# A fused attention and mixture-of-experts layer: normalised rows kept as half-precision pairs and turned by DMA instead of by TensorE

## The chip, the cores and the metric

The kernel runs on one core of one Trainium2 chip. The metric is the device time in microseconds (us) of one execution; the median of several runs counts. The profile that is read here is of one profiled execution of the same program.

## The reference, cut to what matters

4096 tokens of 128 channels pass through a linear attention layer without softmax (16 heads of 8, rotary positions, a causal mask inside each 1024-token sequence, a gate and a layer norm), then a residual and a layer norm, and then a mixture of experts with two of eight experts per token and one shared expert, and again a residual and a layer norm:

```
x  = layernorm(x + attention(x))                    # called x1 below
logits = x1 @ gate_w                                # [4096, 8]
top_v, top_i = top_k(logits, 2);  top_p = softmax(top_v)
combine[t, e] = top_p of token t for expert e, else 0
g = x1 @ Wg[e];  u = x1 @ Wu[e];  d = (silu(g) * u) @ Wd[e]     # 352 inner
expert_out = sum over e of combine[:, e] * d
shared = (silu(x1 @ Sg) * (x1 @ Su)) @ Sd                       # 176 inner
out = layernorm(x1 + expert_out + shared)
```

## The kernel before

The work is cut into 32 tiles of 128 tokens, and four tiles in a row are a quad (R = 4). The five engines run programs of their own that wait for each other on semaphores; their order is written out by hand.

**Attention loop.** Steps s = 0 to 37 are software-pipelined: in step s TensorE (PE) runs `bank_p(s)`, then `proj(s + 3)`, `attend(s - 1)`, `energies(s)`, `products_of(s)` and `turn(s + 1)`. `bank_p` is all that goes into PSUM bank `b_p`: the router's logits of tile s - 5 (L558 to L560), the ranks of a quad's choices (L568 to L573), the transpose of the normalised tile s - 4 (L580), and the output projection of tile s - 2 (L583). ScalarE (ACT) squares the projected tile (L788), copies the turned x1 of tile s - 4 out of PSUM as float16 (`x1T_hi`, L778), copies keys, queries and values, and writes x1 of tile s - 3 twice, once for each chosen expert, as float32 rows (`normalise`, L796). VectorE (DVE) masks the energies (L938), subtracts the float16 part of the turned x1 from its float32 value to get a second float16 part (`x1T_lo`, L1000, which waits for L778), adds the residual (L970), takes moments, and chooses experts once per quad (L1017 and on, `choose_first`). With the high and the low float16 part, three float16 matmuls stand for one in float32. GpSimd (POOL) raises variances to the power -1/2 (L1282) and, one quad behind the choice, scatters each token's row of 132 float32 (128 values, destination, weight) by an indirect DMA into the expert's region of the DRAM tensor `rows` (L1288, 64 DMAs). SyncE (SP) only issues DMAs: in this loop the next tile of the transposed input, `xT_ring` (L416), when `turn` has freed a slot of the ring.

**Shared expert.** From step 32 on PE runs `shared_up` and `shared_down` by quads (L600 to L617), partly inside the last steps. DVE adds the result to x1 in `x_sb` (`shared_add`, L1058) and after the last step builds a table (`table`, L1090 to L1114) that says which expert each group of 256 gathered tokens belongs to.

**Expert loop.** 39 slot tiles of 256 gathered tokens. SP reads the tile's place (L436) and loads its rows from DRAM (L442), four tiles ahead (U = 4); the load of tile t waits until the buffer of tile t - 4 was turned and its metadata copied (L441). PE turns the rows of the next tile with two transposes into `b_in` (`slot_turn`, L654), ACT copies them as float16 (L861), DVE subtracts to get the low part (L1174) and copies destination and weight (L1178). PE's order is `up(t)` (18 float16 matmuls, L669 to L671), `slot_turn(t + 1)`, `down(t - 1)` (6 float32 matmuls, shown as 12 passes, L685). `up(t + 1)` waits for L1174 of tile t + 1. On ACT the order in a tile is three `silu` (L869), the copy L861, then `scale` of the tile before (L880); on DVE three multiplications (L1186), L1174, L1178. POOL scatters each scaled result by two indirect DMAs into `ydram` (L1321). PE's program is unrolled; those of ACT, DVE, POOL and SP are loops whose body holds four slot tiles.

**End.** SP waits until all real slot tiles are scattered (L449), loads the results back (L452), and they are summed, normalised and stored (L460).

## Time and profile before

| what | value |
|---|---|
| runs of the kernel, us | 426.48, 423.6, 424.5; median 424.5 |
| the profiled execution's own time | 426.87 us |
| its span | 425.0 us |
| mean granted TensorE clock | 0.959 |
| busy: PE / weight loads / DVE / ACT / POOL | 82% / 64% / 61% / 55% / 55% |

The span is the time from the first to the last instruction that the profile shows. A busy share is that of the whole span: it says which engine has most to do, and not which one is waited for at a given place. "Idle before, releaser" is the time in which an engine waited and what ended it. The loop of attention steps runs until about 200 us, the shared expert until 237, the expert loop until about 400, and the end to 425.

### The profile page before, as it was taken

The numbers are of one execution on the slowest core, as the hardware profiler recorded it, in microseconds if no ns is written. First come the engines' busy times: TensorE is split into PE (matmuls) and PEld (weight loads), VectorE is DVE, ScalarE is ACT, GpSimd is POOL, SyncE is SP. The second block draws the span as 40 slices with busy tenths as digits, with TensorE's granted clock in tenths as the row PEclk, the third lists the DMA queues.
The fourth block names the chain that finished last, engine by engine and source line by source line (L and its number), as shares of the span: only waits on it lengthen the run. The fifth ranks groups of instructions, "written<-read, shape, count | busy, mean of one in ns | idle before, by whom it ended". The sixth has DMA issues, their size and how long they took to land.

```text
span 425.0 us, 12763 instructions
## 1 busy us (share of the span) xinstructions
PE 347.0 (82%) x4172; PEld 271.8 (64%) x4172; DVE 257.6 (61%) x826; ACT 235.0 (55%) x861; POOL 233.5 (55%) x302
## 2 busy tenths in 40 slices
PE   3798888787978887886489898897977979889980
PEld 2476656565756655645347797877977878779730
DVE  1469998978797879787555443333443433434682
ACT  3587779687877868523112354444454444445354
...
DMA packets 32280, 33.47 MB, mean 79 GB/s; under 512 B 4784, under 2 KB 27632, under 8 KB 32080
## 3 DMA queue, kind: packets, MB, share of 16 engines
...
q10 hardware_dynamic: 320, 0.08, 0.1%
...
## 4 chain that ended last, share of the span: by engine, by line
PE 51%; DVE 15%; issue 11%; ACT 10%; another core or an unknown queue 3%; POOL 3%; DMA 2%; SPq 2%; DVEq 1%; ACTq 0%; POOLq 0%
PE b_p L685 9%; PE b_es L671 6%; PE b_es L669 5%; PE b_es L670 4%; DVE masked_energies L938 4%; PE b_in L477 3%; PE b_es L502 3%; ACT turns L763 2%; PE b_es L514 2%; ACT ffn_staged L869 2%; PE b_o L534 2%; DMA x_rows<-ydram 2%; PE b_in L654 1%; PE b_o L528 1%
## 5 line engine op out<-in xcount | busy, mean ns | idle before, releaser
L1321 POOL DMA_INDIRECT ydram<-ffn_staged,slot_meta x78 | 74.9, 960 | 111.6 <-ACT ffn_staged L880 92.1
L1186 DVE TENSOR_TENSOR ffn_staged<-ffn_staged,b_es 128x256 f32<-128x256 f32 x79 | 31.8, 420 | 78.3 <-ACT ffn_staged L869 57.6
L1288 POOL DMA_INDIRECT rows<-x_rows,place x64 | 65.4, 1023 | 16.0 <-issue 13.6
L669 PE MATMUL b_es<-slots_T,w_hi 128*128 128x256 f16 x158 | 45.4, 287 | 19.2 <-DVE slots_T L1174 18.3
L685 PE MATMUL b_p<-w_down,ffn_staged 128*128 (+1 forms) x468 | 58.7, 275 | 1.0 <-issue 1.0
L685 PEld LDWEIGHTS b_p<-w_down,ffn_staged 128*128 128x128 f32 (+1 forms) x468 | 55.3, 191 | 1.2 <-issue 1.1
L869 ACT ACTIVATE ffn_staged<-b_es 128x256 f32<-128x256 f32 x79 | 29.2, 385 | 33.9 <-PE b_es L671 28.3
L763 ACT ACTIVATE turns<-b_turn,const_sb 128x128 f32<-128x128 f32 x128 | 36.5, 368 | 16.6 <-PE b_turn L488 15.9
L671 PE MATMUL b_es<-slots_T,w_lo 128*128 128x256 f16 x158 | 45.4, 287 | 0.0
L670 PE MATMUL b_es<-slots_T,w_hi 128*128 128x256 f16 x158 | 45.3, 287 | 0.0
L880 ACT ACTIVATE ffn_staged<-b_p,slot_meta 128x128 f32<-128x128 f32 x78 | 24.4, 366 | 35.9 <-PE b_p L685 34.1
L938 DVE TENSOR_TENSOR masked_energies<-b_es,const_sb 128x512 f32<-128x512 f32 x64 | 41.0, 680 | 1.8 <-PE b_es L502 1.4
L477 PE MATMUL b_in<-w_raw,xT_ring 128*128 128x384 f32 x64 | 30.6, 564 | 9.2 <-DMA ln_w_b<-in_ln 6.7
L796 ACT ACTIVATE x_rows<-x_plus,x_shift,rstd 128x256 f32<-128x256 f32 x32 | 19.2, 600 | 27.4 <-DVE x_shift L978 27.0
L1253 POOL TENSOR_TENSOR turned_qk<-qk,const_sb 128x256 f32<-128x256 f32 x32 | 26.2, 820 | 13.5 <-ACT qk L738 13.4
L669 PEld LDWEIGHTS b_es<-slots_T,w_hi 128*128 x158 | 16.0, 101 | 23.9 <-issue 21.3
L752 ACT ACTIVATE v_spread<-b_in 64x64 f32<-64x64 f32 x128 | 28.3, 221 | 1.1
L528 PEld LDWEIGHTS b_o<-turns,states 128*128 128x128 f32 x56 | 8.9, 196 | 30.9 <-DVE products L948 25.4
L1280 POOL TENSOR_TENSOR var_eps<-stat,const_sb 128x2 f32<-128x2 f32 x33 | 7.2, 219 | 36.4 <-ACT squares_out L788 36.1
L502 PE MATMUL b_es<-turns 32*64 32x128 f32 x1024 | 25.5, 286 | 1.7 <-issue 1.0
L920 DVE TENSOR_TENSOR roped<-qk,const_sb 128x256 f32<-128x256 f32 x32 | 23.0, 720 | 6.0 <-ACT qk L738 5.9
L528 PE MATMUL b_o<-turns,states 128*128 128x128 f32 x56 | 13.8, 330 | 15.2 <-DVE products L948 12.4
...
## 6 DMA issues: line engine op xcount, KB each, us to landing
ffn_staged<-rows SPq DMA_DIRECT2D x39, 132.0 KB, 2.1
x_rows<-ydram SPq DMA_DIRECT2D x16, 256.0 KB, 6.8
xT_ring<-in_xT SPq DMA_DIRECT2D x32, 64.0 KB, 1.8
...
out<-x_sb SPq DMA_DIRECT2D x8, 256.0 KB, 2.3
...
ydram<-ffn_staged,slot_meta POOLq DMA_INDIRECT x78
```

The source lines that it names most:

```text
L477: nc.tensor.matmul(b_in[:, 0:3 * P], x_t, w_raw[:, :], start=True, stop=True).then_inc(projected, 1)
L502: mm = nc.tensor.matmul(b_es[H * h:H * h + H, g, P * c:P * c + P], keys[g], queries[g][:, 2 * h:2 * h + 2, H * c:H * c + H], start=True, s ...
L669: nc.tensor.matmul(o, w, slots_T[:, j % 2, 0, :], start=True, stop=False)
L670: nc.tensor.matmul(o, w, slots_T[:, j % 2, 1, :], start=False, stop=False)
L671: mm = nc.tensor.matmul(o, wlo, slots_T[:, j % 2, 0, :], start=False, stop=True)
L685: mm = nc.tensor.matmul(y_ps[:, b * P:(b + 1) * P], hidden_T[0:n, k % 2, c, b * P:(b + 1) * P], w_down_flat[0:n, bass.ds(e * (IC * P) + c ...
L763: nc.scalar.activation(turns[:, t % TR, j * P:(j + 1) * P], b_turn[:, P:2 * P], ACT.Copy, scale=C("spread")[:, j:j + 1])
L869: nc.scalar.activation(silu_gate[:, j % 2, c, :], up_banks[j % 2][c][:, 0:SLOTS], ACT.Silu).then_inc(expert_silu_done[c], 1)
L938: nc.vector.tensor_tensor(masked_energies[:, t % 2, 2 * r:2 * r + 2, :].rearrange("p c (b n) -> p c b n", n=H), b_es[:, 2 * r:2 * r + 2, 0 ...
L1186: ins = nc.vector.tensor_tensor(hidden_T[:, j % 2, c, :], silu_gate[:, j % 2, c, :], up_banks[j % 2][c][:, SLOTS:], ALU.mult)
L1288: nc.gpsimd.indirect_dma_start(out=rows, out_offset=bass.IndirectOffsetOnAxis(ap=place[:, t // R, c, t % R:t % R + 1], axis=0), in_=x1_row ...
L1321: nc.gpsimd.indirect_dma_start(out=ydram, out_offset=bass.IndirectOffsetOnAxis(ap=slot_meta[:, j, b, 0:1].bitcast(u32), axis=0), in_=scale ...
```

## The change

The normalised tile is written by ACT in float32 into `x_sb` (in place of the residual input) and as float16 into `x1_quad`, a buffer of two quads; DVE subtracts the two and writes the low float16 part beside it (`rows_lo`). When the fourth tile of a quad is there, SP issues one DMA that transposes the eight 128x128 float16 blocks of the quad into `x1T` (`turn_x1`), and two DMAs that copy the quad's pairs of float16 into the two sets of rows in `x1_rows`, which are then scattered as before: a row is still 528 bytes, with 128 high and 128 low parts where 128 float32 stood. The logits of a quad are computed together, in the step in which its last tile's were. In the expert loop the transposes on PE and the copies on ACT and DVE are gone: a transposing DMA reads 256 rows of 512 bytes from DRAM straight into `slots_T`, and a small second DMA reads destination and weight into `slot_meta`. The `down` results alternate between banks `b_p` and `b_in`.

```diff
-        x1T = sb("x1T", [P, 2, TOKENS], f16)
+        x1_halves = x1_rows[:, :, :, :].bitcast(f16)
+        x1T = sb("x1T", [P, TILES, 2, P], f16)
+        x1_quad = sb("x1_quad", [P, 2, R, 2, P], f16)
...
-        slots_T = sb("slots_T", [P, 2, 2, SLOTS], f16)
+        slots_T = sb("slots_T", [P, U, 2, SLOTS], f16)
...
-        slots_T_ps = b_in[:, 0:SLOTS]
-        y_ps = b_p[:, 0:SLOTS]
+        y_ps = [b_p[:, 0:SLOTS], b_in[:, 0:SLOTS]]
...
+            def turn_x1(t):
+                if not tile(t):
+                    return
+                if t % R == R - 1:
+                    g = t // R
+                    sp.wait_ge(x1_lo_done, t + 1)
+                    both = x1_quad[:, g % 2, :, :, :].rearrange("p t a n -> p t (a n)")
+                    sp.dma_start_transpose(x1T[:, R * g:R * g + R, :, :].rearrange("p t a n -> p (t a) n"), both.rearrange("p t n -> p (t n)")).then_inc(x1T_loaded[g % 2], 16)
+                    for c in range(TOP):
+                        sp.dma_start(x1_halves[:, R * g:R * g + R, c, 0:2 * P], both).then_inc(rows_doubled[g % 2], 16)
...
+                turn_x1(t - 7)
+            for t in range(TILES - 7, TILES):
+                turn_x1(t)
...
-                    sp.wait_ge(slots_turned, t - U + 1)
-                    sp.wait_ge(meta_copied, t - U + 1)
+                    sp.wait_ge(expert_up_done[IC - 1], t - U + 1)
                     sp.wait_ge(table_loaded, 16)
-                sp.dma_start(slot_rows[:, j, :, :], rows[bass.ds(at, SLOTS), :].rearrange("(p b) w -> p b w", p=P)).then_inc(slots_loaded[j], 16)
+                sp.dma_start_transpose(slots_T[:, j, :, :], row_halves[bass.ds(at, SLOTS), 0:2 * P]).then_inc(slots_loaded[j], 16)
+                if exists(t - U):
+                    sp.wait_ge(y_scattered[j], 32 * i)
+                    sp.wait_ge(table_loaded, 16)
+                sp.dma_start(slot_meta[:, j, :, :], rows[bass.ds(at, SLOTS), DEST:DEST + 2].rearrange("(b p) w -> p b w", p=P)).then_inc(meta_loaded[j], 16)
...
-                if tile(s - 5):
-                    pe.wait_ge(x1T_hi_done, s - 4); pe.wait_ge(x1T_lo_done, s - 4)
...
-                if tile(s - 5):
-                    t = s - 5
-                    o = logits_ps[:, (t % R) * EXPERTS:(t % R + 1) * EXPERTS]
-                    xh, xl = x1T[:, 0, t * P:(t + 1) * P], x1T[:, 1, t * P:(t + 1) * P]
-                    nc.tensor.matmul(o, xh, router_w_hi[:, :], start=True, stop=False)
-                    nc.tensor.matmul(o, xl, router_w_hi[:, :], start=False, stop=False)
-                    last = nc.tensor.matmul(o, xh, router_w_lo[:, :], start=False, stop=True)
+                if quad_routed(s) is not None:
+                    g = quad_routed(s)
+                    pe.wait_ge(x1T_loaded[g % 2], 16 * (g // 2 + 1))
+                    for t in range(R * g, R * g + R):
+                        o = logits_ps[:, (t % R) * EXPERTS:(t % R + 1) * EXPERTS]
+                        xh, xl = x1T[:, t, 0, :], x1T[:, t, 1, :]
+                        nc.tensor.matmul(o, xh, router_w_hi[:, :], start=True, stop=False)
+                        nc.tensor.matmul(o, xl, router_w_hi[:, :], start=False, stop=False)
+                        last = nc.tensor.matmul(o, xh, router_w_lo[:, :], start=False, stop=True)
...
-                if tile(s - 4):
-                    pe.wait_ge(x1_done, s - 3)
-                    last = nc.tensor.transpose(x1T_ps, x1_rows[:, s - 4, 0, 0:P], C("identity"))
...
-                pe.wait_ge(x1T_lo_done, R * q + R); pe.wait_ge(x1T_hi_done, R * q + R)
+                pe.wait_ge(x1T_loaded[q % 2], 16 * (q // 2 + 1))
...
-            def slot_turn(i, j, lag):
-                ok, t, k, r = stage(i, j, lag)
-                if not ok:
-                    return
-                pe.wait_ge(slots_loaded[k], 16 * (r + 1))
-                if exists(t - 1):
-                    pe.wait_ge(slots_copied, t)
-                for b in range(2):
-                    mm = nc.tensor.transpose(slots_T_ps[:, b * P:(b + 1) * P], slot_rows[:, k, b, 0:P], C("identity"))
-                mm.then_inc(slots_turned, 1)
...
-                pe.wait_ge(slots_copied, t + 1)
+                pe.wait_ge(slots_loaded[j], 16 * (i + 1))
+                if exists(t - 2):
+                    pe.wait_ge(hidden_done, t - 1)
...
-                if exists(t - 1):
-                    pe.wait_ge(yscaled[(j + lag - 1) % U], i + (j + lag - 1) // U + 1)
+                if exists(t - 2):
+                    pe.wait_ge(yscaled[(j + lag - 2) % U], i + (j + lag - 2) // U + 1)
...
-            def x1T_hi(t):
-                if not tile(t):
-                    return
-                nc.scalar.activation(x1T[:, 0, t * P:(t + 1) * P], x1T_ps, ACT.Copy).then_inc(x1T_hi_done, 1)
...
                 act.wait_ge(x1_shift_done, t + 1)
-                both = x_plus[:, t % 2, :].unsqueeze(1).broadcast_to([P, TOP, P])
-                nc.scalar.activation(x1_rows[:, t, :, 0:P], both, ACT.Identity, scale=rstd[:, 1 - t % 2, 1:2], bias=x1_shift[:, t % 2:t % 2 + 1]).then_inc(x1_done, 1)
+                if t % R == 0 and t >= 2 * R:
+                    act.wait_ge(x1T_loaded[t // R % 2], 16 * (t // R // 2))
+                    act.wait_ge(rows_doubled[t // R % 2], 32 * (t // R // 2))
+                for to in (x_sb[:, t, :], x1_quad[:, t // R % 2, t % R, 0, :]):
+                    ins = nc.scalar.activation(to, x_plus[:, t % 2, :], ACT.Identity, scale=rstd[:, 1 - t % 2, 1:2], bias=x1_shift[:, t % 2:t % 2 + 1])
+                ins.then_inc(x1_done, 1)
...
-            def slots_hi(i, j, lag):
-                ok, t, k, r = stage(i, j, lag)
-                if not ok:
-                    return
-                act.wait_ge(slots_turned, t + 1)
-                nc.scalar.activation(slots_T[:, k % 2, 0, :], slots_T_ps, ACT.Copy).then_inc(slots_hi_done, 1)
...
-                act.wait_ge(expert_y_done, t + 1); act.wait_ge(meta_copied, t + 1)
+                act.wait_ge(expert_y_done, t + 1); act.wait_ge(meta_loaded[k], 16 * (r + 1))
...
-            def x1T_lo(t):
-                if not tile(t):
-                    return
-                dve.wait_ge(x1T_hi_done, t + 1)
-                nc.vector.tensor_tensor(x1T[:, 1, t * P:(t + 1) * P], x1T_ps, x1T[:, 0, t * P:(t + 1) * P], ALU.subtract).then_inc(x1T_lo_done, 1)
+            def rows_lo(t):
+                if not tile(t):
+                    return
+                dve.wait_ge(x1_done, t + 1)
+                nc.vector.tensor_tensor(x1_quad[:, t // R % 2, t % R, 1, :], x_sb[:, t, :], x1_quad[:, t // R % 2, t % R, 0, :], ALU.subtract).then_inc(x1_lo_done, 1)
...
-                if s >= 5:
-                    dve.wait_ge(x1T_hi_done, min(s - 3, TILES)); dve.wait_ge(squares_summed, min(s - 1, TILES))
-                x1T_lo(s - 4)
+                if quad_ranked(s) is not None or quad_routed(s) is not None or quad_second(s) is not None:
+                    dve.wait_ge(squares_summed, min(s - 1, TILES))
...
+                rows_lo(s - 3)
...
-            def evac(i, j, lag):
-                ok, t, k, r = stage(i, j, lag)
-                if not ok:
-                    return
-                dve.wait_ge(slots_hi_done, t + 1)
-                nc.vector.tensor_tensor(slots_T[:, k % 2, 1, :], slots_T_ps, slots_T[:, k % 2, 0, :], ALU.subtract).then_inc(slots_copied, 1)
-                if exists(t - U):
-                    dve.wait_ge(y_scattered[k], 32 * r)
-                    dve.wait_ge(yscaled[k], r)
-                nc.vector.tensor_copy(slot_meta[:, k, :, :].bitcast(i32), slot_rows[:, k, :, DEST:DEST + 2].bitcast(i32)).then_inc(meta_copied, 1)
...
+                    pool.wait_ge(rows_doubled[t // R % 2], 32 * (t // R // 2 + 1))
```

The order of the programs shifts at three places. First SyncE in the attention loop; the rows are the input tiles' DMAs, and in the new kernel those of a quad.

```order
L412 DMA w_down<-in_Wd 96x8x128
L416 DMA xT_ring<-in_xT 128x128 x23
L422 TENSOR_LOAD ends
```

```order
L434 DMA xT_ring<-in_xT 128x128 x2
L428 DMA_TRANSPOSE x1T<-x_quad 128x8x128
L430 DMA x_rows<-x_quad 128x4x256 x2
L434 DMA xT_ring<-in_xT 128x128 x4
L428 DMA_TRANSPOSE x1T<-x_quad 128x8x128
```

Between every four loads of input tiles now stand three DMAs of a quad. Next SyncE in the loop over slot tiles, one tile of before and then one of the change.

```order
L436 TENSOR_LOAD tile_list
L436 ISA x2
L442 ISA [waits table_loaded,meta_copied,slots_turned]
L442 DMA ffn_staged<-rows 128x264
```

```order
L457 TENSOR_LOAD tile_list
L457 ISA x2
L460 REGISTER_ALU
L462 ISA [waits table_loaded,expert_up_done2]
L462 DMA_TRANSPOSE slots_T<-rows 128x2x256
L466 ISA [waits table_loaded,y_scattered2]
L466 DMA slot_meta<-rows 128x2x2
```

One DMA with one pair of waits became two, and the second waits until the results of the slot tile four back are scattered; the next tile's transposing DMA stands behind it. Last TensorE in the expert loop, from the last matmuls of `up` to the first of the next tile.

```order
L671 MATMUL b_o<-slots_T,w_lo 128x256
L654 MATMUL b_in<-const_sb,ffn_staged 128x128 x2
L685 ISA
L685 MATMUL b_p<-w_down,ffn_staged 128x128
```

```order
L682 MATMUL b_o<-slots_T,w_lo 128x256
L696 ISA
L696 MATMUL b_p<-w_down,ffn_staged 128x128
L696 ISA
L696 MATMUL b_p<-w_down,ffn_staged 128x128
```

The two transposes (L654) are gone, and `down` follows `up` directly.

## Rows read from the trace of the kernel before

**Rows 1.** Windows: start:end, length, busy of PE, PEld, DVE, ACT, POOL, clock, DMA
```profile
260.00:280.00 20.00, 17.13 (x143) 15.35 (x144) 7.55 (x24) 9.14 (x29) 9.57 (x10) 0.94 0.23 65
300.00:320.00 20.00, 17.84 (x163) 16.65 (x161) 8.24 (x25) 9.30 (x29) 9.58 (x10) 1.00 0.24 67
```
**Rows 2.** Timeline, 300 to 307 us, PE in the expert loop: start, us
```profile
300.98 0.25 PEld L654 LDWEIGHTS b_in<-const_sb,ffn_staged 128*128 128x128 f32 x2
...
301.20 1.42 PEld L685 LDWEIGHTS b_p<-w_down,ffn_staged 128*128 128x128 f32 x12
...
301.31 1.50 PE L685 MATMUL b_p<-w_down,ffn_staged 128*128 x12
...
302.65 0.27 PE L669 MATMUL b_es<-slots_T,w_hi 128*128 128x256 f16 x1
...
306.17 0.27 PE L669 MATMUL b_es<-slots_T,w_hi 128*128 128x256 f16 x1
```
**Rows 3.** Waits of PE, whole span: us in total, times, longest
```profile
PE b_es L669 <- DVE slots_T L1174: 18.3, 9, 2.5
```
**Rows 4.** Timelines of PE, ACT and DVE around one such wait
```profile
291.57 1.50 PE L685 MATMUL b_p<-w_down,ffn_staged 128*128 x12
295.52 0.28 PE L669 MATMUL b_es<-slots_T,w_hi 128*128 128x256 f16 x1 [2.45 <-DVE slots_T L1174]
...
293.88 0.38 ACT L869 ACTIVATE ffn_staged<-b_turn 128x256 f32<-128x256 f32 x1 [1.75 <-remote]
...
294.63 0.41 DVE L1186 TENSOR_TENSOR ffn_staged<-ffn_staged,b_o 128x256 f32<-128x256 f32 x1
```
**Rows 5.** Timeline, ACT's scaling and POOL's two scatters of one slot tile
```profile
303.49 0.62 ACT L880 ACTIVATE ffn_staged<-b_p,slot_meta 128x128 f32<-128x128 f32 x2 [1.54 <-PE b_p L685]
...
306.13 0.96 POOL L1321 DMA_INDIRECT ydram<-ffn_staged,slot_meta  x1 [0.30 <-issue]
```
**Rows 6.** Chain of waits, 388 to 396 us: start, us, what
```profile
394.26 0.79 DMA ydram<-ffn_staged,slot_meta
```
**Rows 7.** SyncE's instructions: ns min/median/max, first and last start
```profile
L442 SPq DMA_DIRECT2D ffn_staged<-rows x39: 337/338/362, 226.3 to 380.8; - x39
L436 SPq TENSOR_LOAD <-tile_list x39: 114/273/419, 225.6 to 375.6; - x39
```
**Rows 8.** DMA issues by line: count, KB each, median us to landing
```profile
ffn_staged<-rows SPq DMA_DIRECT2D x39, 132.0 KB, 2.1
x_rows<-ydram SPq DMA_DIRECT2D x16, 256.0 KB, 6.8
xT_ring<-in_xT SPq DMA_DIRECT2D x32, 64.0 KB, 1.8
out<-x_sb SPq DMA_DIRECT2D x8, 256.0 KB, 2.3
```
**Rows 9.** Groups: line, count, busy, mean ns, idle before and its releaser
```profile
L580 PE MATMUL b_p<-const_sb,x_rows 128*128 128x128 f32 x32 | 10.2, 320 | 4.0 <-ACT x_rows L796 2.2 <-issue 1.8
L1000 DVE TENSOR_TENSOR x1T<-b_p,x1T 128x128 f16<-128x128 f32 x32 | 9.1, 285 | 11.4 <-ACT x1T L778 10.5 <-ACT squares_out L788 0.5
L796 ACT ACTIVATE x_rows<-x_plus,x_shift,rstd 128x256 f32<-128x256 f32 x32 | 19.2, 600 | 27.4 <-DVE x_shift L978 27.0
```
**Rows 10.** Timeline, the steps around a quad's last tile, 132 to 142 us
```profile
132.83 0.60 ACT L796 ACTIVATE x_rows<-x_plus,x_shift,rstd 128x256 f32<-128x256 f32 x1
134.07 0.54 DVE L920 TENSOR_TENSOR roped<-qk,const_sb 128x256 f32<-128x256 f32 x1
...
139.12 0.17 PE L558 MATMUL b_p<-router_w_hi,x1T 128*128 128x8 f16 x1
```
**Rows 11.** Timeline, the last tile's logits and their first reader
```profile
195.28 0.60 ACT L796 ACTIVATE x_rows<-x_plus,x_shift,rstd 128x256 f32<-128x256 f32 x1 [2.22 <-DVE x_shift L978]
...
198.69 0.17 PE L558 MATMUL b_p<-router_w_hi,x1T 128*128 128x8 f16 x1
...
200.35 0.18 DVE L1017 TENSOR_REDUCE top_logits<-b_p 128x4 f32<-128x32 f32 x1
```

53 lines of the change are left out of this document (24 added, 29 removed).

## The prediction, made before the changed kernel had run

> **What bounds the kernel now.** I read the views in this order: the windows, to see which engine is full in which stage; the timeline of TensorE in one slot tile; the waits, to see what holds it when it is not full; then the same for one attention step; and last the DMA views, since the change moves work there.
>
> In the expert loop the windows show PE busy 17 to 18 of 20 us, DVE, ACT and POOL under half [rows 1]. The timeline gives the period of an undisturbed slot tile: the first matmul of `up` starts at 302.65 and the next tile's at 306.17, so 3.52 us, and PE has no gap in it [rows 2]. Of these, 0.22 are the two transposes (their weight loads start at 300.98, those of `down` at 301.20). The waits show nine gaps of PE before `up`, together 18.3 us, all ended by DVE's subtraction into `slots_T` [rows 3]. One of them, seen on three engines: PE ends `down` by 293.0 and starts `up` at 295.52; ACT stood still for 1.75 us in the middle of its three `silu` (the trace names no engine that released it, "remote"), and everything behind it on ACT and DVE, the copy and subtraction of the slots too, came late [rows 4]. It returns every four slot tiles, once per pass of ACT's loop. So PE bounds this stage, with one pause per pass that comes from ACT by way of the two copies.
>
> The last of the 39 slot tiles are padding. SyncE goes on when the last real result has landed, at 394.26 + 0.79 = 395.05 [rows 6]; counted back from the 78 scatters that is the 35th tile's. The 36th `up` runs before the 35th `down`, so 36 periods of 3.52 (126.7 us) and the gaps lie on the path to the end. In the attention loop no engine is full. DVE waits 10.5 us in all for ACT's copy of the turned x1, and PE waits 4.0 us before the transpose of x1, for ACT's `normalise` or at issue [rows 9].
>
> **The change part by part.** I sum against the profiled execution, 426.87 us; it lies 2.4 above the median of the runs, 424.5, so the forecast is the sum less 2.4.
>
> *Transposes out of the expert loop.* 36 times 0.22: -7.9 us [rows 2].
>
> *The gaps.* `up` of the next tile no longer waits for ACT and DVE. What is late next is `down`, which waits for DVE's third multiplication of the tile that ACT was late with: that one ended at 294.63 + 0.41 = 295.04 [rows 4]. In the new order PE would start `up` at about 292.8 (`down` without the transposes), need 2.0 us, and stand before the next `down` at 294.8 or a little earlier. About 0.5 us per gap stay, so 9 x 0.5 = 4.5 of 18.3: -13.8 us. Bounds: -18.3 (nothing stays) and 0 (ACT's pause grows or moves to where PE feels it fully).
>
> *The copies on ACT and DVE* (float16 copy, subtraction, metadata) go. Neither engine bounds the stage [rows 1]; 0.
>
> *The wait of SyncE.* The small DMA of tile t now waits for the scatter of tile t - 4, and queued behind it is the transposing DMA of tile t + 1, for which `up(t + 1)` waits. With the new period P = 3.52 - 0.22 = 3.30: `down(t - 4)` ends two periods before `up(t)` starts. In the profile a `down` ended at 301.31 + 1.50 = 302.8 [rows 2]; ACT scaled at 303.49, POOL's second scatter ended at 306.13 + 0.96 = 307.1 [rows 5], and landing takes 0.79 us by the one place where it ends a chain [rows 6]: 5.1 us from the end of `down`. SyncE then issues the small DMA (0.34), reads the next tile's place (0.27) and calculates (some 0.4) [rows 7]. From there to the start of `up(t + 1)`, three periods after that `down`, 9.9 - 5.1 - 1.0 = 3.8 us are left. Nothing is lost if the transposing DMA lands within 3.8 us of its issue. If it takes longer, every five slot tiles make one round of this chain, so each further microsecond costs 36 / 5 = 7.2 us.
>
> *How long a transposing DMA takes* the trace does not show. Nearest rows: the plain load of nearly the same bytes lands in 2.1 us; a store of 256 KB, the size of a quad, in 2.3; the sixteen result loads queued together in 6.8 [rows 8]. A transposing one moves 512 of the same 528 bytes of each row, so I see nothing that would make it shorter: 2.1 to 6.8. I take 3.0 for a slot tile, near its twin, and 3.3 for a quad. Both are then covered, with 0.8 us to spare in the expert loop: 0.
>
> The Trainium skill disagrees with itself here. "Advanced Engine Details and Errata", section X-Bar Transpose, says that a transposing DMA is as fast as a regular one, which is the case I take. "VectorE: DVE Perf Modes", section The three transpose paths, gives 1309 ns for one 128x128 block of 16-bit numbers; four blocks one after another would be an estimated 5.2 us per slot tile and more than the period of 3.30. No row here shows which is right; it is rival two.
>
> *The attention step.* PE loses the transpose and its wait. I count the 4.0 us of wait [rows 9]: -4.0. DVE's wait of 10.5 us I count at nothing, since in the same step DVE waits again for POOL's power before it adds the residual. If that is wrong, it gives up to -10.5 more. On ACT one instruction of 600 ns becomes two of half the width and a copy of 128 columns goes; DVE's subtraction only moves to the end of the step. 0.
>
> *The quad's DMA.* The last tile of a quad is normalised by 133.43, DVE is free for `rows_lo` at 134.07 + 0.54 = 134.6 and done by 134.9. The logits for it start at 139.12 [rows 10]: 4.2 us for 3.3 to land. Covered; above 4.2 each microsecond costs up to 8 us (eight quads).
>
> *The input tiles' queue.* SyncE now waits for `rows_lo` and issues three more DMAs before the next input tile, some 1.2 us of issue at 0.34 each and a step's tail, and their 768 KB lie ahead of its 64 KB, which alone lands in 1.8 [rows 8]. A step is about 5 us, so I expect the projection to wait now and then: 7 x 0.5 = +3.5. Bounds 0 and +14 (2 us per quad).
>
> *The last quad.* x1 is ready at 195.88, its low part at about 196.3, landing at 199.6. The logits began at 198.69, but DVE read them only at 200.35 [rows 11]. +1.0.
>
> Sum: -7.9 - 13.8 - 4.0 + 3.5 + 1.0 = -21.2. 426.9 - 21.2 = 405.7; on the scale of the median 403.3, and I forecast 403.
>
> **The rivals.**
>
> *One, slower: SyncE's chain sets the pace.* If the transposing DMAs take as long as the result loads, 6.8 us, the expert loop gives back (6.8 - 3.8) x 7.2 = 21.6 and the quads 8 x (6.8 - 4.2) = 20.8: 403 + 42 = 446. The place is the start of `up`, waiting for the slots' DMA behind the small one. It turns the gain to a loss from where 7.2 (X - 3.8) + 8 (X - 4.2) = 21.2, X = 5.4 us. For it: no transposing DMA in the trace, the wait for the scatter in front. Against it: the engines of the DMA are busy only 0.24 of the time here [rows 1] and the bytes do not grow.
>
> *Two: the rate, not the delay.* If one transpose must end before the next begins, the period of a slot tile is at least its duration: at 6.8 us instead of 3.3 it is 36 x 3.5 = 126 more, over 540. The Trainium skill's 1309 ns per block is this case; by that page's figure an estimated 5.2 us would be the period.
>
> *Three: the pauses stay.* ACT's pause comes from its loop and not from what it waits for; if it grows or hits `down`, the 13.8 do not come: 417. For it: its releaser is not an engine. Against it: the next `down` has 2 us of `up` in front of it.
>
> *Four: partly exposed.* A slot DMA of 4.5 to 5.5 us gives 403 + 5 to 403 + 22, so 408 to 425, at the top of it no change.
>
> **How the numbers follow.** A measurement of this kernel tells about 1% from no change. Forecast, transfers covered and the gaps mostly gone, 392 to 412: 0.45. Three, 412 to 420: 0.15. Four: 0.18, of which 0.08 lies under 420.3 and 0.10 within 1%. One: 0.14. Two: 0.08. Faster by over 1%: 0.45 + 0.15 + 0.08 = 0.68; within 1%: 0.10; slower: 0.22. The range starts at 391, where the gaps vanish and half of DVE's wait comes back too, and goes to 450, rival one with a little to spare; above lies rival two. The forecast's own range is 392 to 412.
>
> **What would show it.** Right: the period on PE in the expert loop 3.30 us; PE's waits there end with DVE (`hidden`) before `down` and are under 1 us; the transposing DMAs of the slots land within 3.8 us, those of the quads within 4.2; the waits list shows next to nothing for PE on DMAs. Wrong: a group of waits "PE b_es <- DMA slots_T" of 20 us or more (rival one or two: two if the landings follow each other at the pace of the period), a wait of the logits' first matmul on `x1T`, the input projection waiting for `xT_ring`, or the nine gaps still at 2 us before `up` or `down` (rival three).

## The result, and where the time went

The changed kernel takes 431.4 us, median of 4 runs (428.9 to 433.1); the kernel before, run beside it on the same chip, 424.9 (423.6 to 426.5). The ratio is 1.019, 95% interval 1.014 to 1.024: slower, where 403 us and a gain were forecast. Timed again in two later groups of runs, on two different chips, the same kernel gave 1.007 (1.001 to 1.013) and 1.008 (1.002 to 1.014). These ratios take of each kernel only its fast executions, those within 1.5% of its fastest; by the medians of all executions the changed kernel lay under the kernel before in both later groups (429.0 for 432.0 and 428.7 for 434.8 us), where only 9 and 4 of the 29 executions of the kernel before count as fast. So what is firm is that the forecast gain of 5% did not come; a loss of 1.9% was measured once, and how large it is in general, or whether there is one, stays open.

The profiled execution lasted 431.0 us, its span is 428.8. I cut both spans at points that both traces have: the last input projection, the first `up`, the first load of results, and the end. SyncE is released by the last real scatter in both. In the kernel before it goes straight on to the first result load. In the changed one it issues its last small DMA there (393.13) and comes to the result load later, which makes a stretch of its own.

| stretch (us) | before | after | difference |
| --- | --- | --- | --- |
| start to last input projection | 162.8 | 173.8 | +11.0 |
| to the first `up` | 74.5 | 78.0 | +3.6 |
| to the landing of the last real scatter | 157.8 | 141.3 | -16.5 |
| from there to the first result load | 0.0 | 3.3 | +3.3 |
| to the end | 29.9 | 32.4 | +2.5 |

Three of the cuts, as the timelines of PE and SyncE have them (the number behind the start is the duration), first before, then after:

```profile
162.84 0.81 PE L477 MATMUL b_in<-w_raw,xT_ring 128*128 128x384 f32 x2
237.29 0.28 PE L669 MATMUL b_es<-slots_T,w_hi 128*128 128x256 f16 x1 [0.87 <-DVE x_sb L1058]
...
395.09 2.04 SPq L452 DMA_DIRECT2D x_rows<-ydram  x4
```
```profile
173.84 0.91 PE L501 MATMUL b_in<-w_raw,xT_ring 128*128 128x384 f32 x2 [0.32 <-DMA xT_ring<-in_xT]
251.87 0.28 PE L680 MATMUL b_es<-slots_T,w_hi 128*128 128x256 f16 x1 [0.87 <-DVE x_sb L1054]
...
393.13 0.39 SPq L466 DMA_DIRECT2D slot_meta<-rows  x1
396.41 0.82 SPq L476 DMA_DIRECT2D x_rows<-ydram  x2
```

The expert loop gained, as it should; the other stretches lost more than that. Line numbers of the changed kernel: input projection L501, `products` of VectorE L944, low part `rows_lo` L996, quad's transposing DMA L428, its two copies L430, input tile L434, logits L582, `up` L680 to L682, `down` L696, slots' transposing DMA L462, small DMA L466.

**The expert loop.** The timeline of PE in an undisturbed tile answers to [rows 2]: 306.40 - 303.10 = 3.30 us for the 3.52 of before.

```profile
303.10 0.27 PE L680 MATMUL b_es<-slots_T,w_hi 128*128 128x256 f16 x1
...
306.40 0.27 PE L680 MATMUL b_es<-slots_T,w_hi 128*128 128x256 f16 x1
```

The waits of PE answer to [rows 3]: the 18.3 us on `slots_T` from VectorE are gone, and 9.4 us on the slots' DMA and 2.4 us on `hidden` (L1170) have come.

```profile
PE b_o L552 <- DVE products L944: 20.6, 21, 1.8
PE b_es L680 <- DMA slots_T<-rows: 9.4, 12, 1.5
...
PE b_in L501 <- DMA xT_ring<-in_xT: 6.1, 4, 2.2
PE b_in L729 <- DMA x_rows<-ydram: 5.9, 1, 5.9
...
PE b_p L582 <- DMA x1T<-x_quad: 3.4, 1, 3.4
...
PE b_in L696 <- DVE ffn_staged L1170: 2.4, 6, 0.5
```

One trace of each kernel carries some chance. The changed expert loop, with its SyncE part as it is, took 144.5 to 149.1 us (first `up` to first result load) in twelve traces; the old loop took 157.8 here, 162.3 in `e_before_fill` and 152.3 in `e_attention` (two kernels that are described below; the second computes other values). TensorE's granted clock differs as well: 0.97 over the loop before, 1.00 after, 0.94 in `e_before_fill`. The sum had no such term. Before, TensorE is busy for 139.4 of the 157.8 us, so 3% of them, an estimated 4.7 us of the 16.5, may be the clock and not the work that went; no run separates the two.

**The attention stage** stands in the same list. Before, the wait on `products` was 12.4 us and there was none on `xT_ring` or `x1T`:

```profile
PE b_o L528 <- DVE products L948: 12.4, 16, 1.4
...
PE b_in L719 <- DMA x_rows<-ydram: 2.0, 1, 2.0
```

The timelines of SyncE and PE show one wait on `xT_ring` from both sides. SyncE issues the transposing DMA (1.26 us) and the two copies (1.41), and only then the next input tile; PE had ended its projection of the output at 123.2 and stood until 125.31.

```profile
117.90 1.26 SPq L428 DMA_TRANSPOSE x1T<-x_quad  x1
119.21 1.41 SPq L430 DMA_DIRECT2D x_rows<-x_quad  x2
120.66 2.51 SPq L434 DMA_DIRECT2D xT_ring<-in_xT  x2
```
```profile
118.25 0.81 PE L501 MATMUL b_in<-w_raw,xT_ring 128*128 128x384 f32 x2
...
122.53 0.68 PE L604 MATMUL b_p<-rhs,gated_out 128*128 128x256 f32 x2
125.31 1.65 PE L501 MATMUL b_in<-w_raw,xT_ring 128*128 128x384 f32 x2 [2.10 <-DMA xT_ring<-in_xT]
...
128.65 1.91 PE L526 MATMUL b_es<-turns 32*64 32x128 f32 x32
```

Behind that wait the same projection takes 1.65 us for 0.81. The windows (length, busy of PE, PEld, DVE, ACT, POOL, granted clock, DMA share, GB/s) say why: the granted clock fell to 0.50, the lower of TensorE's two levels, 1.2 for 2.4 GHz, for some 10 us. A wait of this length does not always bring the fall: in two later traces of the same kernel TensorE stood 2.32 and 2.05 us (`e_changed_again`, at 54.6 and 122.3) and 2.15 us (`e_changed_third`, at 125.3) for the same DMA, and its clock stayed at 1.00. The first row shows the quad's transfers at 0.85 of the DMA engines.

```profile
120.00:124.00 4.00, 3.21 (x86) 2.44 (x84) 2.76 (x8) 3.88 (x18) 3.34 (x6) 1.00 0.85 211
124.00:128.00 4.00, 2.69 (x22) 1.97 (x26) 3.83 (x12) 1.68 (x9) 3.66 (x6) 0.61 0.16 49
128.00:132.00 4.00, 3.94 (x65) 2.88 (x58) 2.49 (x8) 1.35 (x5) 1.41 (x2) 0.50 0.06 18
132.00:136.00 4.00, 4.00 (x51) 3.05 (x57) 1.89 (x9) 3.39 (x14) 0.96 (x3) 0.61 0.07 20
```

The second new cost is on VectorE. In the kernel before the subtraction (L1000) stood in the middle of the step, where VectorE waited for ScalarE (1.34 us here). It now stands at the end of the step, directly ahead of the masks and `products`, for which PE waits. Timelines of DVE, before and after, and of PE after:

```profile
111.83 1.28 DVE L938 TENSOR_TENSOR masked_energies<-b_es,const_sb 128x512 f32<-128x512 f32 x2
113.03 0.41 DVE L948 TENSOR_TENSOR products<-b_es,const_sb 128x256 f32<-128x256 f32 x1
114.78 0.29 DVE L1000 TENSOR_TENSOR x1T<-b_p,x1T 128x128 f16<-128x128 f32 x1 [1.34 <-ACT x1T L778]
```
```profile
117.59 0.28 DVE L996 TENSOR_TENSOR x_quad<-x_sb,x_quad 128x128 f16<-128x128 f32 x1
117.80 1.28 DVE L934 TENSOR_TENSOR masked_energies<-b_es,const_sb 128x512 f32<-128x512 f32 x2
118.99 0.41 DVE L944 TENSOR_TENSOR products<-b_es,const_sb 128x256 f32<-128x256 f32 x1
```
```profile
119.46 0.49 PE L552 MATMUL b_o<-turns,states 128*128 128x128 f32 x2 [0.40 <-DVE products L944]
```

The groups that answer to [rows 9]: the low part takes 465 ns for 285 in the mean and waits next to nothing (2.3 us, before 11.4); `normalise` is two instructions, 493 and 478 ns, for one of 600.

```profile
L803 ACT ACTIVATE x_sb<-x_plus,x_shift,rstd 128x128 f32<-128x128 f32 x32 | 15.8, 493 | 24.3 <-DVE x_shift L974 23.9
L803 ACT ACTIVATE x_quad<-x_plus,x_shift,rstd 128x128 f16<-128x128 f32 x32 | 15.3, 478 | 0.0
L996 DVE TENSOR_TENSOR x_quad<-x_sb,x_quad 128x128 f16<-128x128 f32 x32 | 14.9, 465 | 2.3 <-ACT x_quad L803 2.3
```

The mean of 465 ns hides two kinds. The median is 292 ns, as before (291, none above 292). Nine of the 32 took 0.43 to 1.30 us. They are just those that began while a two-operand instruction of POOL on 128 or more columns ran, and each ended some 0.15 us after it; `e_changed_again` shows the same in eight of 32. One of them, on POOL and on DVE:

```profile
122.85 0.92 POOL L1235 TENSOR_TENSOR turned_qk<-qk,const_sb 128x256 f32<-128x256 f32 x1
123.12 0.81 DVE L996 TENSOR_TENSOR x_quad<-x_sb,x_quad 128x128 f16<-128x128 f32 x1
```

In the kernel before the subtraction read one operand from PSUM (`b_p`); now it reads both from SBUF. That this difference is why it can be held up is what the trace suggests; no run tests it.

**SyncE's issues** answer to [rows 7] (ns min/median/max, first and last start). The plain slot load was issued in 0.34 us; a transposing one takes 1.2, on the queue that also carries the input tiles.

```profile
L462 SPq DMA_TRANSPOSE slots_T<-rows x39: 512/1207/2130, 241.4 to 389.8; - x39
...
L428 SPq DMA_TRANSPOSE x1T<-x_quad x8: 1260/1266/1363, 49.2 to 211.2; - x8
```

In the first slot tiles, where nothing holds SyncE, its transposing DMAs start at 244.03, 246.62 and 249.21: one slot tile every 2.6 us, for the 3.30 in which PE uses one up. In the twelve places where PE stood waiting for the slots, its first `up` matmul came 2.8 to 4.3 us after the start of that tile's issue (four of them over 3.8 us).

How long a quad takes to land shows at the last one, where PE stands waiting (timelines of SyncE and PE): 214.33 - 211.19 = 3.1 us from issue to the first reader.

```profile
211.19 1.29 SPq L428 DMA_TRANSPOSE x1T<-x_quad  x1
214.33 0.10 PEld L582 LDWEIGHTS b_p<-router_w_hi,x1T 128*128 128x128 f16 x1 [3.86 <-DMA x1T<-x_quad]
```

**Behind the slot loop.** The chain of waits after the loop's last small DMA is SyncE alone: that DMA's issue, then four loads of the counts of scatters into registers and their arithmetic (L470), 3.3 us in all. Before, SyncE did them ahead of a wait of 10.9 us for the last results. Now its wait for the scatters stands ahead of them, inside the loop, in front of the small DMA.

```profile
393.13 0.39 SPq L466
...
393.57 0.29 SPq L470
...
396.01 0.15 SPq L470
...
396.41 0.35 SPq L476
```

### The profile page after: what moved, and what is told of

The parts are those of the page before. It is cut to its first block, busy times and chain, and to the rows that moved or that the text cites. A ratio compares the mean times of both kernels' runs of the same rounds, so it can differ in the third digit from the quotient of the medians.

```text
span 428.8 us, 12467 instructions
## 1 busy us (share of the span) xinstructions
PE 346.8 (81%) x4062; PEld 265.5 (62%) x4062; DVE 243.3 (57%) x748; ACT 224.0 (52%) x822; POOL 234.7 (55%) x302
## 4 chain that ended last, share of the span: by engine, by line
PE 35%; issue 15%; DVE 13%; SPq 11%; DMA 10%; ACT 9%; POOL 3%; another core or an unknown queue 2%; DVEq 0%; ACTq 0%; POOLq 0%
SPq L462 3%; PE b_es L526 3%; PE b_o L558 3%; DVE masked_energies L934 3%; PE b_in L501 3%; ACT turns L773 3%; DMA ydram<-ffn_staged,slot_meta 3%; DMA slots_T<-rows 2%; PE b_es L538 2%; DMA xT_ring<-in_xT 2%; PE b_o L552 2%; DMA x_rows<-ydram 2%; SPq L466 2%; SPq L457 2%
## 5 line engine op out<-in xcount | busy, mean ns | idle before, releaser
L1170 DVE TENSOR_TENSOR ffn_staged<-ffn_staged,b_es 128x256 f32<-128x256 f32 x79 | 30.7, 419 | 58.7 <-ACT ffn_staged L868 35.4
L680 PE MATMUL b_es<-slots_T,w_hi 128*128 128x256 f16 x158 | 43.3, 274 | 10.7 <-DMA slots_T<-rows 9.4
L501 PE MATMUL b_in<-w_raw,xT_ring 128*128 128x384 f32 x64 | 32.4, 593 | 15.7 <-DMA ln_w_b<-in_ln 6.9
L681 PE MATMUL b_es<-slots_T,w_hi 128*128 128x256 f16 x158 | 43.0, 272 | 0.5 <-issue 0.5
L682 PE MATMUL b_es<-slots_T,w_lo 128*128 128x256 f16 x158 | 43.0, 272 | 0.0
L868 ACT ACTIVATE ffn_staged<-b_es 128x256 f32<-128x256 f32 x79 | 27.4, 394 | 20.4 <-PE b_es L682 14.5
L526 PE MATMUL b_es<-turns 32*64 32x128 f32 x1024 | 29.9, 301 | 2.8 <-issue 2.8
L696 PE MATMUL b_in<-w_down,ffn_staged 128*128 (+1 forms) x228 | 29.4, 278 | 2.6 <-DVE ffn_staged L1170 2.4
L552 PE MATMUL b_o<-turns,states 128*128 128x128 f32 x56 | 14.6, 347 | 20.6 <-DVE products L944 20.6
L696 PE MATMUL b_p<-w_down,ffn_staged 128*128 (+1 forms) x240 | 30.1, 274 | 0.0
L696 PEld LDWEIGHTS b_in<-w_down,ffn_staged 128*128 128x128 f32 (+1 forms) x228 | 26.9, 191 | 4.9 <-issue 4.8
L696 PEld LDWEIGHTS b_p<-w_down,ffn_staged 128*128 128x128 f32 (+1 forms) x240 | 28.4, 191 | 0.2
L803 ACT ACTIVATE x_sb<-x_plus,x_shift,rstd 128x128 f32<-128x128 f32 x32 | 15.8, 493 | 24.3 <-DVE x_shift L974 23.9
L1170 DVE TENSOR_TENSOR ffn_staged<-ffn_staged,b_turn 128x256 f32<-128x256 f32 x19 | 8.0, 421 | 32.6 <-ACT ffn_staged L868 20.3
```

The source lines that it names most:

```text
L501: nc.tensor.matmul(b_in[:, 0:3 * P], x_t, w_raw[:, :], start=True, stop=True).then_inc(projected, 1)
L526: mm = nc.tensor.matmul(b_es[H * h:H * h + H, g, P * c:P * c + P], keys[g], queries[g][:, 2 * h:2 * h + 2, H * c:H * c + H], start=True, s ...
L552: nc.tensor.matmul(outT, states[:, t % SR, :], qT, start=True, stop=False, skip_group_check=True)
L680: nc.tensor.matmul(o, w, slots_T[:, j, 0, :], start=True, stop=False)
L681: nc.tensor.matmul(o, w, slots_T[:, j, 1, :], start=False, stop=False)
L682: mm = nc.tensor.matmul(o, wlo, slots_T[:, j, 0, :], start=False, stop=True)
```

## The experiments

Ratios are against the kernel before, run on the same chip beside the others. There are five such groups of runs, and the chips differ: the kernel before had medians of 424.5, 431.2, 425.4, 432.0 and 434.8 us in them. So kernels are compared by ratio (made as said above, so it is not the quotient of two medians), or by median within a group. "Projection" is the start of the last input projection (before 162.8, after 173.8), "loop" the time from the first `up` to the first result load (157.8, 144.5). Both come from one traced execution per kernel, and three traces of the unedited changed kernel have their projection at 169.1, 171.8 and 173.8: differences of a few us between single traces carry little.

### The two halves apart (first group)

`e_experts`: the kernel before with the new expert loop only.

```diff
+x1_tops = x1_rows[:, :, :, :].bitcast(mybir.dt.bfloat16)
-nc.scalar.activation(x1_rows[:, t, :, 0:P], both, ...
+nc.scalar.activation(x1_tops[:, t, :, 1:2 * P:2], both, ...
```

> The kernel before with the changed expert loop alone: slots turned by DMA, banks for y taken in turn, the small DMA for destinations and weights. x1 is rounded to bfloat16 where it is written to the rows (two tile halves of the rows zeroed in the idle first 7 us), so that rows read as half-precision numbers hold no NaN; the slots' values are other ones than the reference's, their sizes are the same. Theory A (the expert loop gains what was predicted, the attention stage loses it): from the first 'up' to the release of the last real scatter 157.8 us fall to 141, SyncE's tail and the end give back 3 to 6, the total is 408 to 413 us. Theory C (the chain of SyncE and what follows the loop eats most of it even with the attention stage of before): 418 us or more.

Measured: 416.2 us, ratio 0.982 (0.973 to 0.992); projection 164.1, loop 145.3, end after the first result load 31.3 us. That is 3 us above theory A's range and 2 under theory C's; the expert half gains, less than theory A said. 

`e_attention`: the kernel before with the new attention stage only.

```diff
-x1T = sb("x1T", [P, 2, TOKENS], f16)
+x1T = sb("x1T", [P, TILES, 2, P], f16)
+x1_quad = sb("x1_quad", [P, 2, R, 2, P], f16)
...
```

> The kernel before with the changed attention stage alone: pairs of halves in a buffer of quads, one transposing DMA and two copies per quad, logits by quads; the expert loop still turns its slots on TensorE, reading the pairs of halves as if they were 32-bit numbers, so that its values are other ones than the reference's. Theory A: the last input projection is issued at 172 to 175 us (162.8 before), the first 'up' at 250 to 253, and the total is 425 + 14 to 15 = 437 to 442 us. If the loss of the attention stage hung on the expert part (its longer code, other banks), it would stay at 425 to 430.

Measured: 433.6 us, ratio 1.021 (1.012 to 1.030); projection 172.4, first `up` 249.6. The loss up to the first `up` comes with the attention half alone, whatever runs behind it; the total stayed 3 us under the range of theory A. The product of the two ratios, 0.982 x 1.021 = 1.003, lies somewhat below the whole change (1.007 to 1.019).

### Input tiles ahead of the quad's DMAs (first and fifth group)

```diff
-    turn_x1(t - 7)
-for t in range(TILES - 7, TILES):
+    turn_x1(t - 8)
+for t in range(TILES - 8, TILES):
     turn_x1(t)
```

> The changed kernel with one number other: SyncE issues the next input tile before it waits for a quad's low part and issues the quad's three DMAs (turn_x1(t - 8) for turn_x1(t - 7)). Theory A (input tiles stand behind the quad's DMAs on SyncE, TensorE waits for them some 2 us once in a quad and then runs at the lower clock level): the waits 'b_in <- DMA xT_ring' vanish (6.1 us to under 1), the last input projection comes at 163 to 166 us instead of 173.8, the total falls by 7 to 11 to 420 to 424 us. Theory B (VectorE's dearer low part, 465 ns for 285, and the logits by quads pace the stage): within 2 us of the changed kernel, 429 to 433 us.

> The changed kernel with the input tile issued ahead of the quad's DMAs and nothing else (the kernel of e_inputs_ahead). Theory A (the queue): 3 to 6 us under e_changed_third. If the earlier ratio of 1.0006 was the chip's and not the edit's: within 2 us of it.

Measured: 425.1 us, ratio 1.001 (0.995 to 1.006), projection 167.6; again, on another chip, 428.5 us, ratio 1.006 (0.999 to 1.013), projection 167.4. The changed kernel beside the second had 428.7 us, ratio 1.008, projection 171.8. The waits on `xT_ring` are gone altogether, but those on VectorE took their place:

```profile
PE b_o L552 <- DVE products L944: 28.7, 25, 1.9
...
PE b_es L680 <- DMA slots_T<-rows: 6.5, 11, 1.0
```

6.1 us of wait went and 8.1 came (28.7 for 20.6). The stage is 4 to 6 us shorter in the traces, while beside the changed kernel the total moved by 0.3 us only. Theory A as the sole cause falls (its 3 to 6 us under the changed kernel did not come): with the queue out of the way TensorE waits for VectorE instead.

### The place and the length of the low part (first and second group)

`e_low_short`: 8 of 128 columns of the low part; the rest of the low halves is left out (zero).

```diff
-nc.vector.tensor_tensor(x1_quad[:, t // R % 2, t % R, 1, :], x_sb[:, t, :], ...
+nc.vector.tensor_tensor(x1_quad[:, t // R % 2, t % R, 1, 0:8], x_sb[:, t, 0:8], ...
```

> The changed kernel with VectorE's low part computed for 8 of 128 columns (the rest stays zero, so the low halves of the rows are left out): 32 operations of 465 ns become about 80 ns, 12 us less work on VectorE over the stage. Theory A: the last input projection stays within 3 us of 173.8, total 427 to 432 us. Theory B (VectorE paces): the stage is 8 to 12 us shorter, total 419 to 423 us.

Measured: 425.7 us, ratio 1.001 (0.995 to 1.007), projection 166.8. The projection came earlier than theory A allowed and the total stayed above theory B's range: VectorE's instruction is on the path, for part of the loss.

`e_low_idle`: input tiles ahead, and three of four low parts back in the old place.

```diff
 rope_add(s + 2)
+if (s - 4) % R != R - 1:
+    rows_lo(s - 4)
 add_x(s - 2)
...
-rows_lo(s - 3)
+if (s - 3) % R == R - 1:
+    rows_lo(s - 3)
```

> e_inputs_ahead with VectorE's low part of three tiles in four moved from the end of its step (right ahead of the masks that TensorE's products wait for) to the place where the subtraction stood before the change, ahead of x_plus in the next step, where VectorE waits for another engine anyway; a quad's last tile stays at the end of its step. Theory D (the cost of the low part is its place, not its length: it stands ahead of the masks): the waits 'b_o <- DVE products' fall from 28.7 us by at least 5, the last input projection comes at 163 to 165 us (167.95 in e_inputs_ahead), total 421 to 423 us. Theory B (its length, 465 ns for 285): no change, 167 to 169 us and 425. Theory E (the quad steps themselves, logits of four tiles ahead of one projection): no change either, but 'x_plus <- POOL rstd' keeps its 9.7 us between 40 and 160 us.

Measured: 424.7 us, ratio 0.991 (0.987 to 0.996), the first version here that lies under the kernel before. The waits on `products` fall from 28.7 to 20.0 us, as theory D wanted. The projection of its trace, 168.5, did not come earlier, as it should have; the granted clock between 120 and 160 us was 0.88 there and 0.96 in the trace of `e_inputs_ahead`, and the traced execution, 426.5 us, was the second longest of twelve. Theory E's sign is absent: 'x_plus <- POOL rstd' fell from 9.7 to 7.5 us. The two kernels ran on different chips; the test of the place side by side stands in the fourth group.

`e_both_short`: the short low part and the input tiles ahead.

> e_inputs_ahead and e_low_short in one (low halves left out but for 8 columns). The two single runs gained 6.3 and 7.0 us of the attention stage. If they are two causes: the last input projection comes at 160.5 to 163 us, total 417 to 420 us. If the short low part only made the quad's DMAs earlier, so that both runs removed one and the same wait: 166 to 168 us and 424 us.

Measured: 424.6 us, ratio 0.997 (0.992 to 1.002), projection 168.2. That is the second expectation (one and the same wait, 166 to 168 us and 424), by 0.2 us missed in the trace; two separate causes, 417 to 420 us, it was not. By ratio it lies under either edit alone (1.001 each), inside the intervals.

### SyncE in the expert part (second group)

`e_loop`: two edits to SyncE, the small DMA one tile later and the counts loaded ahead of the loop. `e_best`: both of them on top of `e_low_idle`.

```diff
+sp.wait_ge(table_made, 3)
+real = [sp.value_load(real_scatters[0:1, k:k + 1], ...) for k in range(U)]
 for k in range(R):
     sp.wait_ge(rows_scattered[k], 32 * QUADS)
...
-sp.wait_ge(y_scattered[j], 32 * i)
-sp.dma_start(slot_meta[:, j, :, :], ...
+load_meta(i, j, -1)
```

> The changed kernel with two edits on SyncE in the expert part: the small DMA of a slot tile (destinations and weights, which waits for that buffer's scatters) is issued behind the transposing DMA of the next tile, and the wait for the table and the loads of the scatter counts stand ahead of the slot loop. Theory C1 (the wait for the scatters, taken between two transposing DMAs, holds the next tile's up): 'b_es <- DMA slots_T' falls from 9.4 us to under 2. Theory C2 (the loads of the counts stand behind the loop): the first result load follows the last scatter's release by under 0.3 us instead of 3.4. Both: the stretch from the first 'up' to the first result load falls from 144.5 to 134 to 138 us and the total to 421 to 426 us. If SyncE's chain itself sets the pace (transposing DMA and small DMA in series), slots_T stays at 9 us and only the 3.4 us come back.

> The changed kernel with all edits that keep its result: input tiles ahead of the quad's DMAs, the low part of three tiles in four in the old place, the small DMA one tile later, the scatter counts loaded ahead of the loop. If the causes add up (theories A, D, C1, C2): last input projection 163 to 165 us, loop stretch 134 to 138 us, total 410 to 415 us, 2 to 3% under the kernel before. If the expert loop then waits for something else (ACT's pauses), 415 to 420 us.

Measured: `e_loop` 432.1 us, ratio 1.013 (1.006 to 1.020), loop 146.9; `e_best` 428.1 us, ratio 0.998 (0.993 to 1.003), loop 151.5. Waits on `slots_T` were 6.9 and 10.0 us. Theory C1 is wrong: the wait for the scatters between two transposing DMAs is not what holds them. On one chip `e_best` is 3.4 us slower than `e_low_idle`, although it has the counts loaded ahead, so the small DMA one tile later costs time by itself. It needs a second load of the tile's place. Where nothing holds SyncE, `e_best` issues its transposing DMAs at 244.40, 247.51 and 250.66, one slot tile every 3.1 us for the 2.6 of the changed kernel: next to PE's 3.30 hardly anything is left to catch up with. So it is SyncE's own chain that has little slack. Theory C2 is right: the timeline of SyncE in `e_loop` ends with

```profile
394.11 1.61 SPq L478 DMA_DIRECT2D slot_meta<-rows  x2
395.89 2.25 SPq L486 DMA_DIRECT2D x_rows<-ydram  x5
```

where 3.3 us lay between the last small DMA and the first result load. From here on only that edit is kept ("tail"). With it and without the later small DMA (`e_ahead_tail_fill1` and `e_best_fill1`) the distance is 0.6 and 0.7 us.

### TensorE's clock (third and fifth group)

Filler: products of which nothing is used, put where PE waits for VectorE. The wait for `gated` moves ahead of the wait for the products with them.

```diff
+if tile(t - 1):
+    pe.wait_ge(gated, t)
+for n in range(2):
+    nc.tensor.matmul(b_o[:, P:2 * P], rhs2[:, 0:P], rhs2[:, 0:P], ...)
 pe.wait_ge(products_masked, t + 1)
...
-if tile(t - 1):
-    pe.wait_ge(gated, t)
```

> The changed kernel with two filler products (128x128, 32-bit, into 128 columns of a bank that nobody reads) in each attention step, put where TensorE waits for VectorE's products anyway. They compute nothing that is used. Over the kernels so far, with the same attention code, the last input projection came at 174.3, 172.8 and 169.9 us where TensorE had run at the lower clock level in 6, 5 and 3 stretches of some 3.4 us: 1.5 us per stretch, 165.3 us with none. Theory F (a good part of the loss is TensorE's clock, which falls where TensorE waits): the low stretches up to the last input projection fall to 0 to 2 and it comes at 166 to 169 us in spite of the filler's own 0.43 us where a step has no wait. Rival (the clock is granted by chance or by another cause, the chain of the step alone decides): stretches stay 3 to 6, and the filler adds up to 5 us.

> The kernel before with the same two filler products per step. It had 2 low stretches before the last input projection (163.2 us). Theory F: 0 to 1 stretches and 161 to 164 us, total 420 to 425 us: little to gain here, which is why the two kernels differ in clock. Rival: the filler costs its own time, 165 to 170 us.

> The changed kernel, unedited, beside the two below on one chip: 1.005 to 1.02 of before.

> The changed kernel with one filler product per attention step and nothing else. If the lower clock is a good part of the loss: 5 to 8 us under e_changed_third (1.2 to 2%). If the clock only follows the waits and costs nothing itself: within 2 us, or slower by the filler.

Measured: `e_fill` 424.1 us, ratio 0.996 (0.992 to 1.001); `e_before_fill` 425.1 us, ratio 1.003 (0.998 to 1.008), projection 161.4. In the fifth group, side by side, the changed kernel 428.7 us (1.008) and one filler product 428.0 us (1.004, 0.996 to 1.011). With two products the clock stayed at the upper level until the last projection (window of `e_fill`, to be held against 0.87 for the same window of the changed kernel):

```profile
120.00:160.00 40.00, 33.14 (x593) 25.80 (x595) 35.12 (x109) 31.18 (x128) 28.59 (x42) 1.00 0.25 66
```
```profile
120.00:160.00 40.00, 33.31 (x574) 24.75 (x572) 31.23 (x99) 28.67 (x119) 27.60 (x40) 0.87 0.28 73
```

That projection came at 169.5 us, though, no earlier than in the changed kernel's own trace of the fourth group (169.1). The rule of 1.5 us per low stretch, on which the expectation was built, does not hold: the fifth group's trace of the changed kernel had two low stretches and its projection at 171.8, the fourth group's had three and 169.1. With one product the trace has the same two low stretches as the changed kernel beside it, and the projection at 172.0; the kernel before with two products kept its two as well. What is left is the time. Two products gave 0.996 where the changed kernel has 1.007 to 1.019, in other groups; one product, side by side, moved the median by 0.8 us, where 5 to 8 were expected, and the ratio by half a per cent, inside the intervals.

One thing more is on record in favour of theory F: over its twelve executions the changed kernel had a mean granted clock of 0.952, with one product 0.964, and in every kernel run ten times or more the executions with the lower clock were the longer ones (correlations of -0.51 to -0.83). That does not say which of the two is the cause: a clock that falls where TensorE waits would give the same picture. So theory F is not shown. That the clock makes a part of the loss agrees with the sign of these numbers; no run here proves it or gives its size.

### The causes together (third and fourth group)

`e_fill_best`: tiles ahead, low part in the old place, tail, two filler products. `e_best_fill1`: the same with one. `e_ahead_fill`: tiles ahead and two. `e_ahead_tail_fill1`: tiles ahead, tail, one; it is `e_best_fill1` without the edit to the low part.

> The changed kernel with input tiles ahead, the low part of three tiles in four in the old place, the scatter counts loaded ahead of the loop, and the filler. By the count of low stretches, e_low_idle and e_best would have had their last input projection at 158.3 us at full clock (168.8 with 7 and 170.3 with 8 stretches). Theory F: 0 to 2 stretches, 159 to 162 us, first 'up' at 233 to 238 us, total 408 to 415 us, 2 to 4% under the kernel before. Rival: 168 to 173 us, total 424 to 430 us.

> The changed kernel once more, unedited, on the chip of the three below. Both theories: 1.5 to 2% above the kernel before; low stretches before the last input projection between 3 and 6, and that projection at 169 to 175 us.

> e_fill (two filler products per step) with the input tile issued ahead of the quad's DMAs. If the queue costs its own time even at full clock (five waits of up to 2.3 us): the last input projection comes 4 to 6 us before e_fill's 169.9, at 164 to 166 us, ratio to before 0.983 to 0.988. If the queue hurt only by letting the clock fall: 168 to 170 us, ratio 0.994 to 0.998.

> Input tile ahead, scatter counts loaded ahead of the loop, one filler product per step, the low part at the end of each step as in the change. If the place of the low part does not matter at full clock, it equals e_best_fill1 within 1 us; if it does, it is 3 to 5 us slower up to the last input projection.

> e_fill_best with one filler product per step instead of two. If one product keeps the clock up as well (0 to 2 low stretches): the filler's own cost halves, the last input projection comes at 161 to 165 us (169.8 in e_fill_best), total 411 to 415 us, ratio to before 0.97 to 0.98. If one is too little: 4 to 8 low stretches, 167 to 170 us, ratio 0.985 to 0.995.

| kernel | median us | ratio (95%) | traced execution, us | projection | loop |
| --- | --- | --- | --- | --- | --- |
| `e_fill_best` (third group) | 416.4 | 0.982 (0.976 to 0.988) | 421.9 | 169.5 | 145.7 |
| `e_changed_again` | 429.0 | 1.007 (1.001 to 1.013) | 425.7 | 169.1 | 147.3 |
| `e_ahead_fill` | 426.5 | 0.994 (0.989 to 0.998) | 428.7 | 170.6 | 146.9 |
| `e_ahead_tail_fill1` | 424.2 | 0.990 (0.986 to 0.995) | 421.5 | 169.1 | 143.1 |
| `e_best_fill1` | 418.2 | 0.976 (0.971 to 0.982) | 418.1 | 164.7 | 144.0 |

The lower four ran on one chip. Against what was expected: `e_fill_best` missed theory F's projection (159 to 162 us) and its total by 1.4 us; `e_changed_again` lost less than half of what was expected; `e_ahead_fill` came out as the queue that costs no time of its own (0.994), not as the one that does; `e_best_fill1` met its projection and ratio, though not its 411 to 415 us.

One edit, the place of three low parts in four, makes 424.2 - 418.2 = 6.0 us between two kernels that are alike otherwise. In the traces 4.4 us of it lie before the last projection (169.1 to 164.7); the trace of the first has about 7 us at the lower clock before that point, that of the second none, so this is not the wait alone. It is the greatest single effect found. The input tiles are ahead in both, so what the place costs with the tiles behind, as in the change itself, no run shows. PE's waits in `e_ahead_tail_fill1`, then in `e_best_fill1`:

```profile
PE b_o L554 <- DVE products L946: 22.5, 23, 1.6
```

```profile
PE b_o L554 <- DVE products L946: 11.3, 13, 1.4
...
PE b_es L682 <- DMA slots_T<-rows: 4.6, 7, 2.2
...
PE b_p L584 <- DMA x1T<-x_quad: 3.5, 1, 3.5
```

The tail edit shows in the loop column: 143.1 and 144.0 for 146.9 and 147.3 us. `e_best_fill1` computes all that the kernel before computes. It is 2.4% faster than that kernel by its ratio, and 2.5% faster than the changed kernel by the two medians (418.2 for 429.0).

## Why the prediction was wrong, step by step

The sum said -21.2 us; the two traces differ by +3.8. The 25.0 us between them, each part rounded: 5.2 in the expert loop (-16.5 for -21.7), 14.1 up to it (+14.6 for +0.5), 5.8 behind it (nothing was forecast there).

*Transposes out of the loop, -7.9:* right. The period fell from 3.52 to 3.30 us.

*The gaps, 4.5 of 18.3 left:* the mechanism was right, the size off. Some 12 us are left, 9.4 on the slots' DMA and 2.4 on `hidden`, where I had reckoned with `hidden` alone. Together with the line above the loop gained 16.5 us for 21.7, and an estimated 4.7 of the 16.5 may be TensorE's clock, which the sum left out; that share of the gain would be luck. `e_experts` shows this half by itself: 0.982.

*SyncE's chain, 3.8 us of slack, cost 0:* this step failed too, by 9.4 us. The chain was followed through one wait only. What it left out is that SyncE needs 2.6 us for each slot tile even when nothing holds it, 1.21 of them for the issue of the transposing DMA, where the plain load's took 0.34. Of 3.30 us that leaves 0.7 to catch up with after a delay. And the slots came 2.8 to 4.3 us after the start of the issue, for the 3.0 assumed. The slack was used up twelve times, at most by 1.5 us. Rival one in full (6.8 us) did not come. Rival two did not come either (its own 126 us make 529; "over 540" holds only with the quads' share added). A quad was readable 3.1 us after its issue began. It is eight blocks of 128x128; at 1309 ns each they would take an estimated 10.5 us. So of the Trainium skill's two statements, the 1309 ns of "VectorE: DVE Perf Modes", The three transpose paths, is not what each further block cost in this queue. That of "Advanced Engine Details and Errata", X-Bar Transpose, that a transposing DMA is as fast as a regular one, is nearer: 2.8 to 4.3 us here for the 2.1 of the plain load. Of the difference 0.9 us is the dearer issue (1.21 for 0.34).

*The quad's DMA, 3.3 of 4.2 us:* right (3.1; a wait only at the last quad). *The last quad, +1.0:* mis-sized, the wait was 3.4 us.

*The input tiles' queue, +3.5 ("some 1.2 us of issue at 0.34 each"):* mis-sized. The three issues take 1.26 + 1.41 = 2.7 us. The waits on `xT_ring` are 6.1 us and lie within the bounds given. The half clock for some 10 us that followed one of them stood nowhere in the sum; it did not follow equal waits in other traces.

*"DVE's subtraction only moves to the end of the step. 0":* this is the step that failed most. It moved from a place where VectorE waited anyway to one that TensorE waits for. The wait on `products` grew from 12.4 to 20.6 us, and to 28.7 when the queue was cleared. Putting three of four back was worth 6.0 us where it was tested, with the input tiles ahead, the tail edit and one filler product. It also ran into POOL nine times, for up to 1.30 us instead of 0.29; what that costs no run tests. The -4.0 for PE's wait ahead of the transpose of x1 cannot be found in the time either: that wait is gone, and the stage is longer all the same.

*Left out altogether:* the loads of the counts behind the loop, +3.3, which SyncE had done beside a wait that the change moved ahead of them; shown by the tail edit. PE's wait for the first results, 5.9 us for 2.0 before, holds the same delay: with the tail edit it is 2.7 and 3.2 us. The end behind the first result load, +2.5, was not tested by itself.

Against the list of what would show the forecast wrong: the input projection waiting for `xT_ring` was named and came, and so did the wait of the logits on `x1T`, once; the 20 us on the slots' DMA did not come; the wait on VectorE's `products` was not on the list.

What stays open: the attention stage of one and the same changed kernel ended between 169.1 and 173.8 us in three traces, which neither the count of low stretches nor the waits explain; whether the clock is a cause of the loss at all, and of how much; and how the +11.0 us before the last projection divide between the queue, the place of the low part and the clock.
